# A fused Flamingo block on one core: start-up loads regrouped, q/k norms by a GpSimd power, encoder values copied by ScalarE

## What is computed

```python
def l2(x): return x * rsqrt(sum(x * x, -1) + 1e-8)          # per head, 16 heads of 8

# L0 cross attention: no softmax, squared scores of normed q and k
q, k, v = ln(x) @ Wq.T + bq, ctx @ Wk.T + bk, ctx @ Wv.T + bv
x = x + tanh(g_xattn[0]) * (((l2(q) @ l2(k).T) ** 2 @ v) @ Wo.T + bo)
# L0 feed-forward: inputs and weights rounded to 4-bit floats in blocks of 16
h = silu(fp4(ln(x)) @ fp4(w_gate).T) * (fp4(ln(x)) @ fp4(w_up).T)
x = x + tanh(g_ffn[0]) * (fp4(h) @ fp4(w_down).T)
# L1 cross attention: one head of 128, masked softmax over ctx
x = x + tanh(g_xattn[1]) * attention(ln(x), ctx, mask)
# L1 encoder layer on ln(x): self attention (16 heads), then 8 experts, top 2 of them
y = layernorm(s + (softmax(q4 @ k4.T / sqrt(8)) @ v4) @ fwo + fbo) * ln1_g + ln1_b
y = layernorm(y + moe(y)) * ln2_g + ln2_b
x = x + tanh(g_ffn[1]) * y
```

## Time and profile before

| | |
|---|---|
| median of 3 runs | 783.88 us (783.53 to 791.24) |
| profiled execution | 783.26 us, of it span 781.5 us |
| busy: TensorE, VectorE, ScalarE, GpSimd | 666.8, 537.4, 413.9, 214.9 us |
| mean granted clock of TensorE | 0.938 of 2.4 GHz |
| instructions | 18070 |

### The profile page before, as it was taken

How to read it: one execution, slowest core, us unless ns; L and a number is a source line. 1 busy time by engine, 2 the same in 40 slices (tenths; PEclk the granted TensorE clock), 3 DMA queues, 4 the chain that set the end, 5 groups by cost and what they waited for, 6 DMA issues and landing times.

```text
span 781.5 us, 18070 instructions
## 1 busy us (share of the span) xinstructions
PE 666.8 (85%) x7536; PEld 459.8 (59%) x7536; DVE 537.4 (69%) x1150; ACT 413.9 (53%) x680; POOL 214.9 (28%) x543
## 2 busy tenths in 40 slices
PE   1249467698789999999999999999999999998983
PEld 0225226456556776676577676676776776575652
DVE  1351644869887877698888887988778857555422
ACT  1242432475575576765756575647574664654431
POOL 4040202224351132243133322233224032221302
PEclk9956757699999999999999999999999999999998
DMA  4510000010000000000000100000000000000000
GB/s 134 137 34 2 28 1 2 0 36 3 1 28 3 1 22 8 2 29 16 1 3 2 34 2 2 2 22 8 3 15 1 2 2 15 1 3 11 4 14 13
DMA packets 23968, 12.60 MB, mean 16 GB/s; under 512 B 6408, under 2 KB 23376, under 8 KB 23888
## 3 DMA queue, kind: packets, MB, share of 16 engines
q1 hardware_dynamic: 23888, 11.45, 5.4%
HBM read 9.35 MB, written 2.10 MB: 15 GB/s over the span
## 4 chain that ended last, share of the span: by engine, by line
PE 71%; DVE 12%; ACT 6%; POOL 4%; SPq 3%; issue 3%; DMA 1%; POOLq 0%; DVEq 0%
PE A L858 19%; PE B L858 15%; PE Y L858 14%; PE H L858 13%; PE B L1101 3%; PE A L862 2%; PE B L862 2%; ACT A L378 1%; ACT hid L378 1%; PE A L997 1%; DVE stats L588 1%; POOL hs L316 1%; DVE qk L658 1%; ACT xn L383 1%; DVE hh L686 1%
## 5 line engine op out<-in xcount | busy, mean ns | idle before, releaser
L858 PE MATMUL H<-xmT,w_s 128*128 128x512 f32 x256 | 137.2, 618 | 7.1 <-ACT hid L378 7.0
L378 ACT ACTIVATE hid<-H,b_s 128x512 f32<-128x512 f32 x128 | 87.7, 686 | 97.6 <-PE H L858 97.2
L306 POOL TENSOR_TENSOR hs<-stats 128x4 f32<-128x4 f32 x48 | 14.7, 305 | 441.6 <-DVE stats L588 441.5
L858 PEld LDWEIGHTS Y<-w_s,hid 128*128 128x128 f32 x1024 | 121.4, 192 | 22.5 <-issue 18.4
L858 PE MATMUL Y<-w_s,hid 128*128 128x128 f32 x1024 | 126.5, 277 | 2.9 <-ACT hid L378 1.6
L835 DVE SCALAR_TENSOR_TENSOR acc<-Y,wgt,acc 128x128 f32<-128x128 f32 x256 | 71.8, 343 | 47.7 <-PE Y L858 47.4
L858 PE MATMUL A<-hT,kT 32*64 32x256 f32 x512 | 49.7, 462 | 9.6 <-ACT A L378 3.7
L858 PEld LDWEIGHTS H<-xmT,w_s 128*128 128x128 f32 x256 | 39.4, 189 | 30.7 <-ACT hid L378 16.9
L858 PE MATMUL A<-wguT,xTq 128*128 128x352 f32 x128 | 49.9, 516 | 8.7 <-DVE hh L686 4.9
L776 DVE TENSOR_REDUCE mx<-B 128x16 f32<-128x1024 f32 x32 | 39.2, 1224 | 22.6 <-PE B L858 22.4
L378 ACT ACTIVATE A<-A 128x1024 f32<-128x1024 f32 x32 | 32.7, 1023 | 36.4 <-PE A L858 36.3
(11 more groups left out here) (192 smaller groups left out, 1311.3 us busy)
## 6 DMA issues: line engine op xcount, KB each, us to landing
xin<-in_x_dram SPq DMA_DIRECT2D x8, 256.0 KB, 3.2
cin<-in_ctx_dram SPq DMA_DIRECT2D x8, 256.0 KB, 3.6
out_dram<-xb SPq DMA_DIRECT2D x8, 256.0 KB, 2.3
w_s<-in_L_ffn_W_dram SPq DMA_DIRECT2D x1, 1024.0 KB
min_<-in_mask_BxSxS_ik_dram SPq DMA_DIRECT2D x8, 128.0 KB, 3.2
hh<-in_L_ffn_w_down_dram SPq DMA_DIRECT2D x1, 176.0 KB, 4.5
rows<-in_L_ffn_ln_g_dram SPq DMA_DIRECT2D x2, 64.0 KB, 6.0
rows<-in_L_ffn_ln_b_dram SPq DMA_DIRECT2D x2, 64.0 KB, 6.1
```

The lines of the kernel that those rows point to most:

```text
L306: pl.tensor_tensor(w[:, 0], st[:, :, 1], st[:, :, 4], ALU.subtract)
L378: return act.activation(dst, source, f, **kw)
L858: return pe.matmul(o, l, r, start=start, stop=stop)
```

## The change

Three things are edited, and ORDER is written anew for every engine.

1. *Loads.* ld_0 is split: three weights (ld_w, for a_w), three biases (ld_b, for a_k), output weight and bias (ld_o), gates (ld_g). ScalarE issues the gates and the seven feed-forward weights on its own queue before its first activation. The rest becomes two items of the sync engine's list: l_1 (18 loads for the second attention and the encoder layer) behind ctx of group 1, and l_e (6 loads for gate and experts) behind the third mask load. s_gate and e_hid of group 0 wait for ld_e; c_kv:0 and s_ob:0 wait for ld_1.
2. *Norms.* Steps 1 to 12 of a_l2 go. GpSimd's new item a_rs adds 1e-8 to the 128 sums and raises them to -0.5; a_l2's last step waits for it.
3. *Encoder values.* s_v4 moves to ScalarE as two plain copies. Since the softmax weights of a row sum to one, the bias fbv may be added after attention: s_ob multiplies it once by fwo on TensorE and VectorE adds the product to the row fbo.

The core of the diff:

```diff
-                for i, w in enumerate((wq0, wk0, wv0, wo0)):
-                    sp.dma_start(raw0[:, i, :], w).then_inc(ld_0, 16)
...
+                for i, w in enumerate((wq0, wk0, wv0)):
+                    sp.dma_start(raw0[:, i, :], w).then_inc(ld_w, 16)
+                for i, v in enumerate((bq0, bk0, bv0)):
+                    sp.dma_start(rows[:, i, :], row(v)).then_inc(ld_b, 16)
+                sp.dma_start(raw0[:, 3, :], wo0).then_inc(ld_o, 16)
+                sp.dma_start(rows[:, 3, :], row(bo0)).then_inc(ld_o, 16)
                 load_x(1, 0)
+                def l_1(g, k):
...
+                def l_e(g, k):
...
+                def a_rs(g, k):
+                    pl.wait_ge(v_l2, 2 * g + 1)
+                    pl.tensor_scalar(ss[:], ss[:], 1e-8, None, ALU.add).then_inc(p_rs, 1)
+                    pl.wait_ge(p_rs, 2 * g + 1)
+                    pl.tensor_tensor(rs[:], ss[:], mhalf[:], ALU.pow).then_inc(p_rs, 1)
...
+                act.dma_start(gates[:, 0:2], row(g_xattn)).then_inc(ld_g, 16)
+                act.dma_start(gates[:, 2:4], row(g_ffn)).then_inc(ld_g, 16)
+                for i, w in enumerate((w_gate, w_up)):
+                    for c, (a, n) in enumerate(IC):
+                        act.dma_start(wraw[0:n, (3 * i + c) * P:(3 * i + c + 1) * P], w[a:a + n, :]).then_inc(ld_f, 16)
+                act.dma_start(wraw[:, 6 * P:6 * P + I], w_down).then_inc(ld_f, 16)
+                act.wait_ge(ld_g, 16 * LOADS_G)
...
+                def s_v4(g, k):
+                    filled(act, "s_v4", g)
...
+                    for h in range(2):
+                        rng = slice(64 * h, 64 * h + 64)
+                        last = copy(vz4[rng].rearrange("p x q n -> p x (q n)")
+                                    .rearrange("p x (u v) -> p x u v", v=16)[:, :, 0:4:3, 8 * h:8 * h + 8],
+                                    B20[rng, :].rearrange("p (x q d) -> p x q d", q=2, d=HD))
+                    last.then_inc(free["B2"], 1)
...
-                    ve.wait_ge(v_l2, base + k)
-                    if k == 1:
-                        ve.tensor_scalar(ssh[:], ss[:], 1e-8, 0.5, ALU.add, ALU.mult).then_inc(v_l2, 1)
...
                     else:
+                        ve.wait_ge(p_rs, 2 * g + 2)
                         by8 = qk[:].rearrange("p w t (h d) -> p (w t h) d", d=HD)
                         ve.tensor_tensor(by8, by8, rep(rs[:], 2, HD), ALU.mult).then_inc(v_l2, 1)
...
+                def s_ob(g, k):
+                    pe.wait_ge(ld_1, 16 * LOADS_1)
+                    claim(pe, "s_ob", g)
+                    mm(B1[:, 0:P], cols[:, 4:5].to_broadcast([P, P]), wdir[:, 6, :]).then_inc(full["B1"], 1)
```

More of the change, by code:

```diff
@@ L1195 @@
     "TensorE": """
-        a_ctx:0 a_w:0 a_ctx:1 a_kv:0 a_wo:0 a_n1t:0 a_q:0 f_w:0 f_wd:0 a_kt:0 a_qt:0 a_s0.0:0 a_sh.0:0 a_n1t:1
-        a_s0.1:0 a_sh.1:0 a_av.0:0 a_s0.2:0 a_sh.2:0 a_av.1:0 a_s0.3:0 a_sh.3:0 a_av.2:0 a_av.3:0 a_o0:0 a_q:1
-        a_kv:1 c_kv:0 a_n1t:2 f_qxt:0 f_gu.0:0 a_ctx:2 a_qt:1 f_gu.1:0 f_gu.2:0 a_kt:1 f_gu.3:0 a_s0.0:1 a_sh.0:1
-        a_s0.1:1 a_sh.1:1 a_av.0:1 a_s0.2:1 a_sh.2:1 a_s0.3:1 a_av.1:1 a_sh.3:1 a_av.2:1 a_av.3:1 f_qht:0 f_qhu:0
-        a_o0:1 f_dn:0 a_q:2 a_kv:2 c_n3t:0 c_q1:0 c_s:0 f_qxt:1 f_gu.0:1 a_n1t:3 c_pt:0 f_gu.1:1 c_av:0 a_qt:2
@@ new lines @@
+        a_n1t:1 a_s0.1:0 a_sh.1:0 a_av.0:0 a_s0.2:0 a_sh.2:0 a_s0.3:0 a_av.1:0 a_sh.3:0 a_av.2:0 a_av.3:0 a_o0:0
+        a_kv:1 a_q:1 a_ctx:2 a_n1t:2 f_qxt:0 a_kt:1 f_gu.0:0 a_qt:1 f_gu.1:0 f_gu.2:0 f_gu.3:0 a_s0.0:1 a_sh.0:1
+        a_s0.1:1 a_sh.1:1 a_av.0:1 a_s0.2:1 a_sh.2:1 a_av.1:1 a_s0.3:1 a_sh.3:1 a_av.2:1 a_av.3:1 f_qht:0 f_qhu:0
+        a_o0:1 a_q:2 f_dn:0 a_kv:2 c_n3t:0 c_q1:0 f_qxt:1 c_s:0 f_gu.0:1 a_n1t:3 f_gu.1:1 c_pt:0 c_av:0 a_kt:2
+        a_qt:2 c_kv:1 f_gu.2:1 a_s0.0:2 a_sh.0:2 s_n4t:0 f_gu.3:1 s_k4:0 s_v4:0 a_s0.1:2 a_av.0:2 a_sh.1:2 s_q4:0
@@ new lines @@
+        a_s0.2:2 a_sh.2:2 s_s.0:0 s_sh.0:0 a_av.1:2 a_s0.3:2 a_av.2:2 a_sh.3:2 s_s.1:0 a_av.3:2 s_sh.1:0 a_o0:2
+        a_ctx:3 s_t.0:0 a_kv:3 s_s.2:0 s_sh.2:0 a_q:3 f_qhu:1 f_qht:1 s_av.0:0 s_t.1:0 f_dn:1 s_s.3:0 s_sh.3:0
+        s_av.1:0 s_t.2:0 a_n1t:4 s_av.2:0 s_t.3:0 a_qt:3 a_kt:3 s_av.3:0 f_qxt:2 c_n3t:1 s_o4:0 a_s0.0:3 c_q1:1
+        a_sh.0:3 c_s:1 f_gu.0:2 a_av.0:3 f_gu.1:2 c_pt:1 c_av:1 f_gu.2:2 s_n5t:0 c_kv:2 f_gu.3:2 s_gate:0 e_hid.0:0
+        a_s0.1:3 s_n4t:1 a_sh.1:3 e_hid.1:0 s_k4:1 a_s0.2:3 a_av.1:3 e_hid.2:0 a_sh.2:3 s_v4:1 s_q4:1 a_s0.3:3
@@ new lines @@
+        s_gt:0 a_sh.3:3 a_av.2:3 e_bias:0 s_s.0:1 a_av.3:3 s_sh.0:1 a_o0:3 e_hid.3:0 s_s.1:1 a_ctx:4 e_out.0:0
+        e_hid.4:0 s_sh.1:1 e_hid.5:0 e_out.1:0 s_t.0:1 f_qht:2 e_hid.6:0 s_s.2:1 f_qhu:2 s_sh.2:1 e_out.2:0 a_kv:4
+        e_hid.7:0 a_q:4 s_av.0:1 f_dn:2 s_t.1:1 e_out.3:0 s_s.3:1 s_av.1:1 f_qxt:3 e_hid.8:0 s_sh.3:1 a_n1t:5
+        f_gu.0:3 e_hid.9:0 c_n3t:2 s_t.2:1 f_gu.1:3 c_q1:2 e_hid.10:0 f_gu.2:3 s_av.2:1 s_t.3:1 e_out.4:0 a_kt:4
+        c_s:2 a_qt:4 s_av.3:1 e_hid.11:0 f_gu.3:3 e_hid.12:0 s_o4:1 e_out.5:0 c_pt:2 e_hid.13:0 c_av:2 e_hid.14:0
@@ new lines @@
+        a_s0.0:4 c_kv:3 e_hid.15:0 a_sh.0:4 e_out.6:0 a_s0.1:4 a_ctx:5 a_sh.1:4 s_n4t:2 e_out.7:0 s_n5t:1 a_av.0:4
+        a_s0.2:4 s_gate:1 s_k4:2 a_sh.2:4 e_hid.0:1 a_av.1:4 s_v4:2 s_q4:2 a_s0.3:4 a_av.2:4 s_gt:1 a_sh.3:4 s_s.0:2
+        e_hid.1:1 s_sh.0:2 a_av.3:4 f_qht:3 e_bias:1 e_hid.2:1 a_o0:4 s_s.1:2 f_qhu:3 e_hid.3:1 s_sh.1:2 f_dn:3
+        e_out.0:1 s_t.0:2 a_kv:5 s_s.2:2 e_hid.4:1 s_sh.2:2 a_q:5 e_hid.5:1 s_av.0:2 s_t.1:2 e_out.1:1 s_av.1:2
+        s_t.2:2 e_hid.6:1 e_out.2:1 c_n3t:3 s_s.3:2 a_n1t:6 s_sh.3:2 c_q1:3 e_hid.7:1 f_qxt:4 s_av.2:2 c_s:3
```

386 lines of the change are left out of this document (172 added, 214 removed).

## The result

| | before | changed |
|---|---|---|
| median | 787.4 us (783.5 to 791.2, 4 runs) | **921.6 us** (920.4 to 924.1, 4 runs) |
| ratio of the runs | | **1.171**, interval 1.163 to 1.179 |
| span of the profiled execution | 781.5 us | 918.5 us |
| mean granted clock of TensorE | 0.938 | 0.866 |

The change makes the kernel 17% slower. The forecast was 754 us; the time lies above its range too.

A forecast was written before the change was run, and what follows sets the result against it. TensorE was taken to bound the kernel from 200 to 650 us, with about 79 us idle before that. 783.3 - 24 (head) - 5 (early groups) - 1 (steady stretch) + 0.6 gave 754 us; range 740 to 905 us.

The forecast's parts named there:

- I take 1.3 us: GpSimd's power over 128x128 in a_rs: mostly a fixed cost, 1.3 us, the lower end of 1.3 to 27 us.
- costs by the column: Rival on GpSimd's a_rs: power grows with each column, 27 us, whole kernel 900 us; chance 0.20.
- the factors of the next norm: GpSimd work named as standing behind a_rs's wait; the forecast gave its delay no term.
- 4.4 us a group: Other VectorE work between sum and scaling, averaged over groups 1 to 7, taken to hide the power.
- break-even: Power length at which the 29 us won are lost again: about 8 us.
- The head: Regrouped loads let a_kt:0 on TensorE start at 26.6 instead of 50.45 us: 24 us saved.
- room for two queues at once: Head loads: 123 GB/s at first against 210 GB/s later, so ScalarE's second queue was taken to fit.
- The rival that it would not be: Early groups wait for something else, half the head's gain is lost: 768 to 780 us; chance 0.10.
- What the removed Newton steps are worth: VectorE loses 28.5 us of norm steps: 5 us gained in groups 1 to 3, 1 us in the steady stretch.
- The encoder values: Moving them from VectorE to ScalarE, with the bias through s_ob: 0 us, 1.5 us either way.
- The rule that was weighed: VectorE and GpSimd share an SBUF port pair as an exclusive lock: at most 4 us, 758 instead of 754 us.

The follow-up runs named there:

- a_widths: The changed kernel with the GpSimd power over 4, 8, 16, 32, 64, 96, 112 and 128 columns in groups 0 to 7: 836.3 us (one run).
- a_idle: The changed kernel with VectorE waiting for a 4-column power only, followed on GpSimd by a 124-column power of a constant that nobody reads: 825.4 us, ratio 1.047.
- a_w4: The changed kernel with the power over only 4 of the 128 columns, the other norm factors left out: ratio 0.971.
- a_w24: The changed kernel with the power over only 24 of the 128 columns, the other norm factors left out: ratio 0.991.
- b_loads: The kernel before with the new loads alone, Newton steps and encoder values as before: 769.5 us, ratio 0.972.
- b_head: b_loads with first feed-forward rounding earlier on VectorE, and group 0's turned x and query projection ahead of the output weight: 768.6 us, ratio 0.974.
- b_w4: The kernel before with the Newton steps replaced by a GpSimd power over only 4 of 128 columns: 785.7 us, ratio 0.995.

## Why the prediction was wrong

**The step that failed: "I take 1.3 us".** The power's cost was bounded at 1.3 and 27 us, and I took the lower end, because a plain GpSimd sum has a fixed part and the power "starts from a fixed part too". The row hinted at the opposite and I noted it in the rival: 0.84 us over four columns is much for something fixed. The plain operation in the same form takes 204 ns at 4 columns, so a fixed part of GpSimd of about 0.2 us could be seen, and nothing in the rows said that the other 0.84 us were fixed too. Measured (a_widths): 0.4 us fixed and 0.16 us a column, 20.8 us for a term of 1.3. The upper end of the bound was nearer by far.

**The price of a long power.** The rival "costs by the column" was the right one, and its own arithmetic gives for 20.8 us: 754 + 19.5 in the head + 0.75 x 7 x (20.8 + 0.25 - 4.4) = 87 us, together 861 us. In ratio to the 783.9 us that the forecast started from the changed kernel took 918. The waits in it were right: 16.7 us a group, and 17.1 are measured on average in groups 1 to 7 (142.8 us less the 22.9 of the head); the 107 us asked for them stand against 97, from a_idle to the changed kernel. What failed is that the rival priced VectorE's wait alone. The text named "the factors of the next norm" as what is queued behind a_rs on GpSimd and put that queue at nothing; a_idle prices it at 60 us. Beside that, the 754 us it starts from were 7 us too low (a_w4: 761). 7 - 10 + 60 are the 57 us between 861 and 918. With the range's upper end at 905 us the time fell outside.

For short powers the average failed. 4.4 us a group were to be hidden, so a_w24, with a power of 4.2 us, should have cost nothing over a_w4; it costs 0.020, 16 us. By the forecast's own list groups 0, 1, 4 and 6 have only 2.6, 2.1, 1.0 and 3.1 us of other work, and the 9.8 us of group 3 do not help them. The break-even came out at 5 us and not at 8.

**The head: right mechanism, 5 us too large.** 24 us were forecast, 26.6 us for a_kt:0. In a_w4 and b_loads it starts at 31.36 and 31.61 us, 19 us earlier than before. Two steps of the sum failed. One is the transfers: I wrote that the engines have room for two queues at once, since the mean rate was below the later one. The landing times say otherwise (DMA issues of the first 12 us, size and us from issue to landing, before and then after):

```profile
y<-in_L_xattn_Wv_w_dram SPq DMA_DIRECT2D x1, 64.0 KB, 2.5
```

```profile
y<-in_L_xattn_Wv_w_dram SPq DMA_DIRECT2D x1, 64.0 KB, 6.8
```

ctx of group 0 was used at 8.28 us in the changed kernel and at 7.2 to 7.7 us in b_loads, b_head and a_w4, against 4.84 before, and a_w started at 9.67 instead of the forecast 6. These landing times agree with the Trainium skill, "DMA: Bandwidth & Descriptors", section Issuing engines are not separate DMA queues: transfers issued by different engines run on the same 16 DMA engines and interleave. The other is GpSimd: in a_w4 the norm factors of x of group 1 stood ahead of a_rs and ended at 28.3 us, so the scaling began 5.8 us after the sum and not the 2.6 us of the two rounding steps. The row at 26.58 above shows why they were slow, 2.12 us for a power over 4 columns that takes 1.04, beside a rounding step of two SBUF operands on VectorE (26.48 to 27.80 us). The forecast gave GpSimd no time between the sum and the power in the head.

**The earlier start was passed on.** The rival that it would not be (768 to 780 us) is refuted by b_loads: 18.8 us in the head, 22 us in the whole.

**What the removed Newton steps are worth: right in size, not shown in place.** 6 us forecast, 4 measured (b_w4, 2 to 6 by the interval). 5 of the 6 were to be won in groups 1 to 3. The profiled executions don't show that: the sum of group 3 ends at 201.1 us in b_w4 and at 196.0 before. How far the hit is luck stays open.

**The encoder values: right within the noise.** 0 forecast, 0 to 5 us. ScalarE's busy time, 424 to 434 us forecast, is 421.5; the copies cost 1.0 us a group, below the 1.2 to 2.4 of the bound, so the strided writes did not double them. VectorE's 506.4 us stand against 498, GpSimd's 393.5 against 227.

**The rule that was weighed.** The forecast put at most 4 us on VectorE and GpSimd sharing a port pair as an exclusive lock. For the narrow instructions of the head the trace agrees (2.12 us instead of 1.04). For the long power it does not: the scaling took 1.23 us inside a power of 20.15 us. The Trainium skill, "SBUF — State Buffer", section Who interferes with whom, calls the shared port pair an exclusive lock, and says of VectorE's two-port modes that it is held for the whole instruction. Read so for two SBUF inputs as well, the scaling would have waited until 148.8 us; the measurement decides. What contention these rows show is small: in the changed kernel the eight scalings take 13.0 us together (11.9 before) and the 48 narrow powers 53.1 us (49.9 before), 4.3 us of busy time more, against 134 us lost.

**The clock.** TensorE's mean granted clock fell from 0.938 to 0.866, in the stretches with holes (0.65 from 50 to 200 us, 0.89 to 650). b_loads has 1.00 from 200 to 650 us. It is low where TensorE has holes; how much of the 157 us it adds was not measured by itself.

## What to carry to other kernels

Before an operation is moved to another engine, split the nearest row into its fixed part (a plain operation of the same shape) and the rest, and let the rest grow with the size unless a second size says otherwise. Price a long instruction twice: for the engine that waits for the result, and for all that stands behind it in its own engine's list; here 97 and 60 us. Where an engine's idle time is to hide it, go group by group, since an average hides the groups that have none. And work on an engine that is 83% busy is nearly free when it is spread over its small waits (4 us for 28.5) and costs its full length when it stands in one run before something that the bounding engine waits for (28 us).

## What the runs showed of the hardware

- GpSimd's power: 0.4 us + 0.16 us for each column of 128 partitions, linear from 4 to 128 columns (a_widths). Over a constant it takes as long (124 columns of ones in 20.15 us, a_idle). The forecast's nearest rows were 2.1 ns a column for a sum.
- A long power on GpSimd leaves VectorE's two-operand instructions undisturbed but at its start: 1.23 us in the middle of a power of 20.15 us, 1.34 to 1.47 us within 0.2 us of its start (a_idle). A power over 4 columns took 2.12 us instead of 1.04 beside such an instruction.
- Issuing the feed-forward weights on a second queue doubled the landing time of the 64 KB weights beside them (2.5 to 3.1 us in the kernel before, 5.1 to 6.8 in the changed one, 5.3 to 6.2 in b_loads).
